# Reordering one joined stage of a graph network kernel: sort first on two engines, additions between ranks on the third, the node update behind the loop

## The reference

```python
# layer 0, the end of it: alpha and kv are known per edge, edges are ordered by row
out = segment_sum(alpha[:, :, None] * v[col], row, num_segments=n)   # n nodes x 128
h = x + (out.reshape(n, 128) @ Wo.T + bo)
h = layer_norm(h) * ln_g + ln_b
x = layer_norm(x + h)
# layers 1 to 3 sum over edges grouped by the other end, dst:
out = segment_sum(weight_of_edge * h[src], dst, num_segments=n)
```

## Time and profile before

| | |
|---|---|
| median of 3 runs | 9892.19 us (9885.96 to 9899.58) |
| the profiled execution | 9893.61 us, its span 9891.9 us |
| joined stage, first to last instruction | about 2766 to 4617 us |
| slots with ticks of the sum | 2797.6 to 4301.9 us |
| slots of the sort and the update | 4301.9 to 4616.9 us |
| next stage begins | 4625.3 us |

### The profile page before, as it was taken

One profiled execution on the slowest core, in us unless ns is written; L12 is line 12 of the kernel. 1 busy time (PEld: TensorE's weight loads), 2 busy tenths in 40 slices (PEclk: granted clock), 3 DMA queues, 4 the chain that ended last, 5 costly groups with the idle time before them and its releaser, 6 DMA issues. The chain is left out here.

```text
span 9891.9 us, 126524 instructions
## 1 busy us (share of the span) xinstructions
PE 5812.9 (59%) x33682; PEld 5019.6 (51%) x33682; DVE 5293.0 (54%) x14739; ACT 1940.4 (20%) x3223; POOL 6078.0 (61%) x6199
## 2 busy tenths in 40 slices
PE   6777747777356666674677764577762333433334
PEld 5666637777344444453566663566652333333333
DVE  7666634444755555575477773344454444444445
ACT  0111111111122222210244442344430000000000
POOL 2777727777344444454677761777735777667774
PEclk8555568888656666655899995555555555655556
DMA  0000027777211111101555542343311111121111
GB/s 8 2 2 2 2 83 211 209 209 209 79 43 41 41 41 41 39 11 30 145 137 135 137 108 34 77 79 79 79 33 49 52 52 52 50 56 52 52 52 47
DMA packets 843234, 707.71 MB, mean 72 GB/s; under 512 B 308546, under 2 KB 734276, under 8 KB 842490
## 3 DMA queue, kind: packets, MB, share of 16 engines
q0 software_dynamic: 211680, 354.89, 14.7%
q1 hardware_dynamic: 500604, 287.21, 11.9%
q10 hardware_dynamic: 130584, 61.48, 2.2%
HBM read 608.58 MB, written 94.38 MB: 71 GB/s over the span
## 5 line engine op out<-in xcount | busy, mean ns | idle before, releaser
L1636 PE MATMUL sum_ps_sum<-sum_hot,sum_msg 128*128 128x128 f32 x3528 | 841.9, 431 | 1437.2 <-DVE acc L1605 1367.9
L1636 PEld LDWEIGHTS sum_ps_sum<-sum_hot,sum_msg 128*128 128x128 f32 x3528 | 771.0, 330 | 1508.4 <-DVE acc L1605 1431.5
L568 POOL DMA_INDIRECT payload_dst<-place_dst_pay,place_dst_at_i x882 | 913.1, 1035 | 961.7 <-DVE place_dst_at_i L756 703.4
L1704 POOL DMA_INDIRECT attend_rows<-h_table,dst_other x882 | 872.6, 989 | 515.5 <-issue 267.2
L1580 POOL DMA_INDIRECT sum_rows<-x_table,dst_other x882 | 847.3, 961 | 485.2 <-issue 268.6
L440 POOL DMA_INDIRECT payload_src<-load_src_pay_slot,load_src_at_i x882 | 864.2, 980 | 437.7 <-issue 275.6
L1704 POOL DMA_INDIRECT attend_rows<-xl_table,dst_other x882 | 875.6, 993 | 393.2 <-issue 268.7
L1281 POOL DMA_INDIRECT scores_rows<-kv_table,scores_idx x882 | 836.5, 948 | 421.0 <-issue 248.9
L1580 POOL DMA_INDIRECT sum_rows<-conv_table,dst_other x882 | 846.5, 960 | 349.6 <-issue 268.6
L1776 PE MATMUL attend_ps_sum<-attend_hot,attend_msg 128*128 128x128 f32 x3528 | 670.5, 365 | 499.7 <-DVE acc L1937 499.7
L1776 PEld LDWEIGHTS attend_ps_sum<-attend_hot,attend_msg 128*128 128x128 f32 x3528 | 617.2, 270 | 543.6 <-issue 471.9
(11 more groups left out here) (466 smaller groups left out, 13758.4 us busy)
## 6 DMA issues: line engine op xcount, KB each, us to landing
attend_win<-xr_table SPq DMA_DIRECT2D x882, 68.0 KB
scores_win<-q_table ACTq DMA_DIRECT2D x882, 64.0 KB
spill<-scores_rows SPq DMA_DIRECT2D x126, 448.0 KB
place_dst_rows<-spill SPq DMA_DIRECT2D x126, 448.0 KB
attend_rel_all<-rel_flat_dst SPq DMA_DIRECT2D x252, 224.0 KB
payload_src<-load_src_pay_slot,load_src_at_i POOLq DMA_INDIRECT x882
scores_rows<-kv_table,scores_idx POOLq DMA_INDIRECT x882
payload_dst<-place_dst_pay,place_dst_at_i POOLq DMA_INDIRECT x882
```

Of the source, the lines that this page charges most:

```text
L568: pool.indirect_dma_start(o.payload, bass.IndirectOffsetOnAxis(ap=at_i[:, t:t + 1].bitcast(U32), axis=0), pay[:, t, :], None).then_inc(sca ...
L1636: mm = pe.matmul(ps_sum[:, n, j, :], msg[:, n, j, :], hot[:, n, j, :], start=True, stop=True)
L1704: pool.indirect_dma_start(rows[:, g % RING, j, :], None, table, bass.IndirectOffsetOnAxis(ap=o.other[:, t:t + 1].bitcast(U32), axis=0)).th ...
```

## The change

The sum's ticks no longer bunch up. `ticks_by` gives one tick to each of slots 2 to 129, `LAST_SUM` is gone, and the update's 12 ticks take the slots 130 to 141, behind sort and sum alike.

Within a slot, TensorE now takes spread, turn, look-up and tables first and the tick after them; ScalarE copies back before the one-hot. VectorE loads the first columns at the head of the slot, then adds tables and places; the message comes before the additions, and the 7 additions stand between the 7 ranks, one rank and one addition by turns; compare follows them. `place` no longer ends with a wait for its own last instruction; the next `place` waits for it before it overwrites `picked`, and `rank_tile` waits for the place of three groups earlier before it overwrites a rank buffer.

```diff
--- before.py
+++ after.py
@@ -551,12 +551,11 @@
         multiplied, product_used, normed, var_ready, rs_ready = (
             st.sem(n) for n in ("multiplied", "product_used", "normed", "var_ready", "rs_ready"))
 
-        LAST_SUM = 97
         blocks = NC
-        n_slots = R + 4
-        ticks_by = lambda n: min(R + 2, max(0, (n - 2) * (R + 2) // (LAST_SUM - 2)))
+        n_slots = R + 4 + blocks + 3
+        ticks_by = lambda n: min(R + 2, max(0, n - 1))
         sum_ticks = {n: [t - 1 for t in range(ticks_by(n - 1), ticks_by(n))] for n in range(-1, n_slots)}
-        norm_ticks = {LAST_SUM + 2 + 2 * m: m for m in range(blocks + 2)}
+        norm_ticks = {R + 4 + m: m for m in range(blocks + 2)}
         norms_done = lambda m: 2 * min(m, blocks) - (0 < m <= blocks)
 
         with nc.Block() as block:
@@ -673,18 +672,15 @@
                     mm.then_inc(multiplied, 1)
 
                 for n in range(-1, n_slots):
-                    ticks = sum_ticks[n]
-                    if ticks:
-                        sum_tick(ticks[0])
                     if n + 1 < R:
                         spread_keys(n + 1)
                         turn_low(n + 1)
-                    for t in ticks[1:]:
-                        sum_tick(t)
                     if 0 <= n < R:
                         look_up(n)
                     if n + 1 < R:
                         tables(n + 1)
+                    for t in sum_ticks[n]:
+                        sum_tick(t)
                     if n + 1 in norm_ticks and norm_ticks[n + 1] < blocks:
                         products(norm_ticks[n + 1])
 
@@ -711,13 +707,9 @@
                     act.activation(rs[:, n % 2], inverse[:, n % 2], ACT.Sqrt).then_inc(rs_ready, 1)
 
                 for n in range(-1, n_slots):
-                    ticks = sum_ticks[n]
-                    for t in ticks[:1]:
-                        if t + 1 < R:
-                            one_hot(t + 1)
                     if n + 1 < R:
                         low_back(n + 1)
-                    for t in ticks[1:]:
+                    for t in sum_ticks[n]:
                         if t + 1 < R:
                             one_hot(t + 1)
                     if n in norm_ticks:
@@ -747,6 +739,8 @@
 
                 def place(g):
                     dve.wait_ge(looked, g + 1)
+                    if g:
+                        dve.wait_ge(at_ready, g)
                     dve.tensor_tensor(picked[:], hi3[:, g % 3].rearrange("p h g -> p g h"), ps_look[:, :, 0:HB],
                                       ALU.mult).then_inc(picked_read, 1)
                     dve.wait_ge(picked_read, g + 1)
@@ -754,17 +748,17 @@
                     dve.wait_ge(at_summed, g + 1)
                     dve.wait_ge(ranked, G * (g + 1))
                     dve.tensor_tensor(group(at_i, g), at[:], rank[:, g % 3], ALU.add).then_inc(at_ready, 1)
-                    dve.wait_ge(at_ready, g + 1)
-
-                def ranks(g):
-                    dve.wait_ge(keys_spread, g + 1)
-                    if g:
-                        dve.wait_ge(ranked, G * g)
-                    for j in range(G):
-                        t = g * G + j
-                        dve.scalar_tensor_tensor(same[:, j, :], ps_key[:, j, :], pay[:, t, 0:1], c.before[:],
-                                                 ALU.is_equal, ALU.mult,
-                                                 accum_out=rank[:, g % 3, j:j + 1]).then_inc(ranked, 1)
+
+                def rank_tile(g, j):
+                    if j == 0:
+                        dve.wait_ge(keys_spread, g + 1)
+                        if g >= 3:
+                            dve.wait_ge(at_ready, g - 2)
+                        if g:
+                            dve.wait_ge(ranked, G * g)
+                    dve.scalar_tensor_tensor(same[:, j, :], ps_key[:, j, :], pay[:, g * G + j, 0:1], c.before[:],
+                                             ALU.is_equal, ALU.mult,
+                                             accum_out=rank[:, g % 3, j:j + 1]).then_inc(ranked, 1)
 
                 def message(w):
                     dve.wait_ge(rows_in[w % 3], 16 * (w // 3 + 1))
@@ -775,21 +769,18 @@
                                       over_tiles(alpha[:, w * G * heads:(w + 1) * G * heads], D // heads),
                                       ALU.mult).then_inc(msg_ready, 1)
 
-                def additions(w):
+                def first_columns(w):
                     _, base = nc.values_load_multi_w_load_instructions(
                         o0.base[0:1, w * 8:w * 8 + 8], engines=[dve.engine], min_val=0, max_val=N,
                         skip_runtime_bounds_check_because="keys are node numbers")
-                    dve.wait_ge(summed, w + 1)
-                    for j in range(G):
-                        dve.wait_ge(added, 1 + w * G + j)
-                        to = acc[:, bass.ds(base[j], P)]
-                        dve.tensor_tensor(to, to, ps_sum[:, j, :], ALU.add).then_inc(added, 1)
-
-                def sum_tick(t):
-                    if 0 <= t - 1 < R:
-                        additions(t - 1)
-                    if t + 1 < R:
-                        message(t + 1)
+                    return base
+
+                def add(w, j, base):
+                    if j == 0:
+                        dve.wait_ge(summed, w + 1)
+                    dve.wait_ge(added, 1 + w * G + j)
+                    to = acc[:, bass.ds(base[j], P)]
+                    dve.tensor_tensor(to, to, ps_sum[:, j, :], ALU.add).then_inc(added, 1)
 
                 link = Chain(dve, normed)
 
@@ -848,18 +839,28 @@
                 dve.memset(acc[:], 0.0).then_inc(added, 1)
                 for n in range(-1, n_slots):
                     ticks = sum_ticks[n]
+                    w = ticks[0] - 1 if ticks and 0 <= ticks[0] - 1 < R else None
+                    base = first_columns(w) if w is not None else None
                     if 0 <= n < R:
                         add_tables(n)
                     if 0 <= n - 1 < R:
                         place(n - 1)
-                    for t in ticks[:1]:
-                        sum_tick(t)
+                    if ticks and ticks[0] + 1 < R:
+                        message(ticks[0] + 1)
+                    for j in range(G):
+                        if n + 1 < R:
+                            rank_tile(n + 1, j)
+                        if w is not None:
+                            add(w, j, base)
                     if 2 <= n + 2 < R:
                         compare(n + 2)
                     for t in ticks[1:]:
-                        sum_tick(t)
-                    if n + 1 < R:
-                        ranks(n + 1)
+                        if t + 1 < R:
+                            message(t + 1)
+                        if 0 <= t - 1 < R:
+                            base = first_columns(t - 1)
+                            for j in range(G):
+                                add(t - 1, j, base)
                     if n in norm_ticks:
                         norm_tick(norm_ticks[n])
 
```

## The result

The changed kernel takes 9467.2 us in the median (9466.9 to 9471.7, 4 runs), the kernel before beside it 9889.1 (9883.7 to 9899.6, 4 runs): a ratio of 0.9573, with an interval of 0.9557 to 0.959. It is faster, by 422 us where the forecast of 9333 asked for 556. The time is inside the range of 9230 to 9530 and outside the forecast's own one of 9275 to 9400. Beside the experiments further down the kernel before took about 12,100 us instead of 9,890 (medians of 12,094 to 12,187), so each of them stands against runs of the kernel before made beside it.

A forecast was written before the change was run, and what follows sets the result against it. TensorE was to bound the loop at 9.1 us a slot: 121 slots end it near 3938, the update at 4060, the next stage starts at 4064, 561 us off 9893.6, giving 9333 us, range 9230 to 9530.

The forecast's parts named there:

- The ring is cut: In the loop, VectorE's add-tables, place and message no longer stand between TensorE's tables and the additions; `sums` had waited 519.7 us.
- A pair costs 0.49 us: On VectorE, one rank and one addition by turns cost 0.49 us, 3.4 us for seven.
- VectorE's slot of 7.4 us: VectorE's work per slot: add-tables to place 1.93 us, compare 0.96, message 1.08, pairs 3.4; up to 10.7 us.
- Rival A: VectorE becomes the bound: pairs overlap less, first-column loads exposed, 9.7 us a slot; middle price 9470 us, chance 0.14.
- The ring of 7.5 us: From `sums` through fill, spread, seven ranks and additions to the next `sums`: 7.5 us, 10.0 at the upper end.
- TensorE's slot: TensorE's instructions in a row: 8.7 us with a fast look-up, 11.3 at the low clock throughout; taken as 9.1.
- the one in six: Share of TensorE's slots put at the low-clock price, adding 2.6/6 to 8.7 us for 9.1 us.
- its two signs: In the changed kernel's timeline, 9.1 us from spread to spread and TensorE's granted clock near 0.65 to 0.7.
- Rivals B and C: B: TensorE always at low clock, 11.3 us a slot, 9599 us, chance 0.09; C: always at high clock, 9233 us, 0.08.
- Rival D: GpSimd becomes the bound: its scatters stretch and end the stage; at 10.5 us a group 9386 us, chance 0.05.
- Rival E: The ring does not break: add-tables still wait for matmuls behind `sums`, 14.8 us a slot, 10,023 us, chance 0.04.
- One tick per slot, update at the end: Loop of 121 slots at 9.1 us ends at 3938, then 122 us of uncovered update and a barrier of some 4.

The follow-up runs named there:

- the schedule alone: Kernel before with its old order within a slot, but one tick a slot and the update at the end: ratio 1.0103 to the kernel before.
- Bf16 sums: Changed kernel with messages and one-hots held as bf16: ratio 0.9744 to the kernel before, 0.973 when measured again.
- the first pair: The result's own runs, changed kernel beside the kernel before: 9467.2 us beside 9889.1, ratio 0.9573.

## Why the prediction was right, and where it was off

- **The ring is cut**: right. `sums` waits 8.4 us instead of 519.7, and the schedule alone, without the cut, makes the kernel 1.0% slower.
- **A pair costs 0.49 us**: right, 0.46 to 0.48. The prediction had read from the Trainium skill (VectorE: DVE Perf Modes, "Rules for kernel authors": minimize the number of chained operations, not their semaphores) that their order would not matter to their sum. Here it does: the same seven pairs take 3.29 us by turns and 4.7 us apart.
- **VectorE's slot of 7.4 us**: right. It was busy 17.29 of 18 us at slots of 7.58 us, so it could not go much below 7.3, and in the changed kernel, where TensorE has no idle time, it is not the bound. The loads of the first columns leave no gap of 0.84 us. Rival A falls. That its middle price of 9470 us is nearly the measured 9467 is chance: its cause, a busy VectorE, is not what is seen.
- **The ring of 7.5 us**: low, as the message has to wait for `sums` too: 3.35 + 0.1 + 1.09 + 3.29 and the next `sums`' start make about 8.0 (3508.09 to the end of the additions at 3516.07). It is under TensorE's slot. Bf16 sums shorten it with the slot.
- **TensorE's slot, "I put one slot in six at the low price"**: this is the term that was mis-sized. The engine is the bound as forecast, the two prices are near (8.7 against 8.91, 11.3 against 11.02), but about 5 slots in 8 pay the high one: 10.19 us instead of 9.1, and 121 x 1.09 = 132 us of the 134 by which the time is over. I had read the share off look-ups that followed `sums` after a gap; the one in six was a margin on top, which no row gave. With the gap gone, they are slow in most slots (75 of 120); with the gap back (schedule alone) most are fast (78 of 124), but not nearly all. That the gap itself does it is argued from these two, and no run changed the gap alone. The prediction had named this as its weakest point ("if the clock behaves otherwise once TensorE has no gap"), and its two signs missed by it: 10.19 us from spread to spread for 9.1, and a granted clock of 0.56 for 0.65 to 0.7. That the time still lies in the range is owed to the range, which was wide enough for rival A's upper price; the forecast's own ended at slots of 9.65 us.
- **Rivals B and C** are the two ends of that term, and neither came in full: low throughout only with bf16 sums, high throughout nowhere. But the sign that the prediction gave for B, a look-up of 3.2 us in most slots, did come, so the kernel stands between the forecast and B: 134 us above the one and 132 below the other (9599). The sort-only part, which spoke for B, shows TensorE without a gap in the slots of the earlier trace rows only; over the stretch of the earlier trace rows it was busy 211 of 315 us. The Trainium skill's sentence in TensorE: Matmul & The Clock Gate, Part 1, that sustained activity releases the low rate, does not hold in this loop: 1233 us of unbroken matmuls were granted 0.56.
- **Rival D**: the scatters took 1004 ns in the mean, no more than before, and the last one started 138 us before the end. **Rival E**: the ring broke.
- **One tick per slot, update at the end**: 121 us of update for 122 forecast; the barrier 1.2 us for 4. The loop's last addition ends at 4074.4, 136 us after the 3938 forecast, nearly all of it the slot's.

## What to carry to other kernels

Once a ring is cut, the engine that becomes full must be priced by what it does without gaps, and a clock read in slots with gaps is no evidence for slots without. Where a slot's bound is TensorE at the low clock, work is taken from it by the operand: bf16 in place of f32 where precision allows (2.42 us a slot here), and a moving operand without a stride (1.00 us). A total that does not move may hide a slot that does: look at the slots without a stop.

## What the runs showed of the hardware

- TensorE's clock rose just behind the end of some `sums` of f32 and fell again in the tables, in an engine that was never idle (granted 0.56 over 1233 us), and with bf16 sums it stayed at 0.50 through the whole stage.
- The tables' matmuls, whose moving operand had a stride of 7 elements, took 2.37 us with the clock low throughout and 2.36 us where it was still high in their first part; with a contiguous one they took 1.37 at the low clock. With bf16 sums, so with the clock low throughout in both, the mean of one went from 493 to 371 ns. With f32 sums it went from 492 to 328 ns, some of them at the high clock:

```profile
L626 PE MATMUL place_dst_ps_tab<-place_dst_hi,place_dst_lo 128*128 128x350 bf16 x882 | 148.4, 328 | 5.4 <-issue 5.4
```

- In the experiments with a full TensorE its signals came late in about every other slot, several at once, and VectorE and ScalarE waited for them (up to 7.5 us in the rows shown), while GpSimd issued on, with or without 448 KB of loads a slot. In the first pair, and with the schedule alone, no signal for the tables was more than 0.7 us late.
